# Row maxima by 64-row products, probability sums on GpSimd alone, and the division in four pieces, in a 16-head attention on one core

## What is computed

```python
x = layernorm(x + L0_attn(x))   # a test-time-trained attention, 8 chunks of 256 tokens
x = layernorm(x + L0_ffn(x))    # 8 experts, top-1 routing with a capacity
x = layernorm(x + L1_attn(x))   # softmax attention, the part that the change touches
x = layernorm(x + L1_ffn(x))    # 8 gated experts, top-1, and a shared one

def L1_attn(x):                 # 16 heads of 64, s = 2048
    q, k, v = (x @ W).reshape(b, s, 16, 64) for W in (Wq, Wk, Wv)
    dot = einsum('bihd,bkhd->bhik', q, k)
    w = softmax(dot / sqrt(64))
    return einsum('bhij,bjhd->bihd', w, v).reshape(b, s, 1024) @ Wo + bo
```

## Time and profile before

| what | us |
|---|---|
| median of 3 runs (1936.26 to 1939.78) | 1939.38 |
| profiled execution | 1943.69 |
| its span, from first to last instruction | 1942.4 |
| TensorE busy (matmul) | 1715.7 (88%) |
| VectorE busy | 1404.4 (72%) |
| GpSimd busy | 1094.9 (56%) |
| ScalarE busy | 774.3 (40%) |

### The profile page before, as it was taken

The page is one execution under the profiler, slowest core; times in us unless marked ns, Lnnn a source line. Parts: engine busy times, 40 slices in busy tenths (PEclk is TensorE's granted clock), DMA queues, the critical chain, the costliest instruction groups (busy, mean ns, idle before and its releaser), DMA issues.

```text
span 1942.4 us, 35745 instructions
## 1 busy us (share of the span) xinstructions
PE 1715.7 (88%) x13785; PEld 935.6 (48%) x13785; DVE 1404.4 (72%) x2509; ACT 774.3 (40%) x1175; POOL 1094.9 (56%) x644
## 2 busy tenths in 40 slices
PE   5877852848999999999999999999999999996793
PEld 4766641834444444444444444444444444443473
DVE  3576546567787777877777877777788788877575
ACT  2454430423444444444444444434344444442221
POOL 2232202233777777776777777767677777775303
PEclk9978755869999999999999999999999999998797
DMA  7000000210000000000000000000000000002212
GB/s 234 3 3 4 3 1 17 62 29 1 1 1 1 1 1 1 1 1 1 1 1 1 1 1 1 1 1 1 1 1 1 1 1 1 1 1 65 64 41 61
DMA packets 35199, 29.77 MB, mean 15 GB/s; under 512 B 4060, under 2 KB 30928, under 8 KB 35032
## 3 DMA queue, kind: packets, MB, share of 16 engines
q1 hardware_dynamic: 27064, 20.28, 3.6%
q0 software_dynamic: 2048, 4.20, 0.7%
q10 hardware_dynamic: 5920, 3.01, 0.5%
HBM read 18.31 MB, written 9.18 MB: 14 GB/s over the span
## 4 chain that ended last, share of the span: by engine, by line
PE 81%; DVE 9%; issue 5%; POOL 4%; DMA 1%; ACT 1%; SPq 0%; DVEq 0%; POOLq 0%; ACTq 0%
PE psum L1774 23%; PE psum L1759 20%; PE psum L1733 8%; PE psum L1753 6%; PE psum L1789 2%; PE psum L1783 2%; PE psum L1404 2%; PE psum L1706 1%; DVE a_mx L1937 1%; PE psum L1365 1%; PE psum L1180 1%; PE psum L1192 1%; POOL a_acc L2068 1%; PE psum L447 1%; PE psum L452 1%
## 5 line engine op out<-in xcount | busy, mean ns | idle before, releaser
L2068 POOL TENSOR_TENSOR a_acc<-a_acc,a_Pb 128x832 f32<-128x832 f32 x448 | 892.7, 1993 | 311.2 <-ACT a_Pb L1876 277.3
L1937 DVE TENSOR_REDUCE a_mx<-psum 128x2 f32<-128x1024 f32 x512 | 625.7, 1225 | 237.3 <-PE psum L1733 234.3
L1876 ACT ACTIVATE a_Pb<-psum 128x1024 f32<-128x1024 f32 x512 | 496.8, 1022 | 704.4 <-PE psum L1759 701.4
L1774 PE MATMUL psum<-a_Pb,a_Vb 128*64 128x512 f32 x2048 | 494.1, 603 | 0.0
L1988 DVE TENSOR_TENSOR a_acc<-a_acc,a_Pb 128x192 f32<-128x192 f32 x448 | 232.6, 519 | 28.2 <-ACT a_Pb L1876 5.0
L1774 PEld LDWEIGHTS psum<-a_Pb,a_Vb 128*64 128x64 f32 x2048 | 127.0, 136 | 244.5 <-issue 173.6
L1733 PE MATMUL psum<-a_Kh,a_Qh 64*128 64x512 f32 x1024 | 230.9, 447 | 10.6 <-DVE a_mx L1937 10.5
L1759 PE MATMUL psum<-a_Qh,a_Kh 64*128 64x512 f32 x1024 | 231.0, 446 | 0.0
L1733 PEld LDWEIGHTS psum<-a_Kh,a_Qh 64*128 64x128 f32 x1024 | 97.0, 184 | 225.4 <-issue 214.5
L1759 PE MATMUL psum<-a_Ql,a_Kh 64*128 64x512 f32 x1024 | 203.8, 393 | 0.0
L1759 PE MATMUL psum<-a_Qh,a_Kl 64*128 64x512 f32 x1024 | 203.0, 391 | 0.0
(11 more groups left out here) (375 smaller groups left out, 1950.8 us busy)
## 6 DMA issues: line engine op xcount, KB each, us to landing
x_rows<-zero ACTq DMA_DIRECT2D x2, 1472.0 KB, 16.4
g_w<-in_L_ffn_w_eDF_dram SPq DMA_DIRECT2D x2, 1408.0 KB, 9.6
r_W<-in_L_ffn_W_dram SPq DMA_DIRECT2D x1, 2048.0 KB, 11.4
r_tile_x<-x_rows SPq DMA_DIRECT2D x23, 64.0 KB, 1.9
y_rows<-r_tile_y SPq DMA_DIRECT2D x23, 64.0 KB, 1.5
g_tile_x<-x_rows SPq DMA_DIRECT2D x23, 64.0 KB, 1.9
y_rows<-g_tile_y SPq DMA_DIRECT2D x23, 64.0 KB, 1.5
g_w<-in_L_ffn_w_eFD_dram SPq DMA_DIRECT2D x2, 512.0 KB, 11.3
```

Source lines behind the costliest of these rows:

```text
L1774: last = pe.matmul(ps[HEAD[h], B_O, :], b.Vb[:, p // 2 % 2, kc, at], b.Pb[:, step % BUFS, h * QT:(h + 1) * QT], start=(kc == 0), stop=(kc ...
L1876: act.activation(b.Pb[:, step % BUFS, :], ps[:, slot:slot + 2, :].rearrange("p a b -> p (a b)"), ACT.Exp, scale=SCALE).then_inc(S["probs"], 1)
L1937: v.tensor_reduce(b.mx[:, :, qc, quarter:quarter + 1], ps[:, bank:bank + 2, :], AX.X, ALU.max).then_inc(S[f"free{bank}"], 1)
L2068: g.tensor_tensor(b.acc[:, u, at], before, b.Pb[:, step % BUFS, at], ALU.add).then_inc(S["added_pool"], 1)
```

## The change

- The ones products: instead of four of 32 rows for a round there are two of 64 rows for each tile of keys, ahead of that tile's scores, one for each head. The first pair waits for the first probabilities of the round before, the second for the second. Mr and its mask then hold four rows at 0 and four at 64, and negate writes nm once, not twice.
- The constant POOL = 832 goes. VectorE adds nothing any more, and GpSimd adds all 1024 columns, 15 times in a unit. One semaphore, added, replaces two.
- The division is done in four pieces of 128 columns. They stand at the ends of rounds 3, 5, 6 and 7 on VectorE; the reciprocals are in rounds 2 to 5, ahead of the early maximum. At the very end each piece follows its reciprocal.
- The sums of U - 1 are taken in round 1 instead of 2, the output of U - 2 in round 2 instead of 1.
- Two waits of VectorE on its own semaphores are added (negated, normalised).

```diff
--- before.py
+++ after.py
@@ -1552,7 +1552,6 @@
 RN = NT // 2
 ROUNDS = UNITS * RN
 STEPS = 2 * ROUNDS
-POOL = 832
 BUFS = 8
 SCALE = 1.0 / float(np.sqrt(D))
 B_O, B_M, B_P = 4, 5, 7
@@ -1564,10 +1563,10 @@
     p, qt = U // NU, U % NU
     if d == 0 and p < PAIRS - 1:
         return "k", p + 1, qt
-    if d == 1 and U > 1:
+    if d == 1 and U:
+        return "sum", U - 1
+    if d == 2 and U > 1:
         return "out", U - 2
-    if d == 2 and U:
-        return "sum", U - 1
     if d == 3 and p // 2 < PAIRS // 2 - 1:
         return "v", p // 2 + 1, U % RN
     if d == 4 and U < UNITS - 2:
@@ -1746,14 +1745,13 @@
             freed(("mask", U))
             freed(("q", U))
             freed(("k", p, NU - 1))
-        if R:
-            pe.wait_ge(S["probs"], 2 * R)
-        for g in range(4):
-            rows = slice(32 * g, 32 * (g + 1))
-            pe.matmul(ps[:, 2 * (g % 2) + g // 2, :], b.ones[rows, :], b.Mr[rows, :], start=True, stop=False, tile_position=(32 * g, 0))
         for i in range(2):
             kc, slot = 2 * d + i, 2 * i
             at = slice(kc * P, (kc + 1) * P)
+            if R:
+                pe.wait_ge(S["probs"], 2 * R - 1 + i)
+            for h in range(2):
+                pe.matmul(ps[:, slot + h, :], b.ones[HEAD[h], :], b.Mr[HEAD[h], :], start=True, stop=False)
             for n, (K, Q) in enumerate(((b.Kh, b.Qh), (b.Kh, b.Ql), (b.Kl, b.Qh))):
                 for h in range(2):
                     last = pe.matmul(ps[:, slot + h, :], K[HEAD[h], p % 2, at], Q[HEAD[h], U % 3, :], start=False, stop=(n == 2))
@@ -1776,15 +1774,14 @@
             last.then_inc(S["weighted"], 1)
 
     def sums(U):
-        pe.wait_ge(S["added_dve"], 15 * (U + 1))
-        pe.wait_ge(S["added_pool"], 15 * (U + 1))
+        pe.wait_ge(S["added"], 15 * (U + 1))
         bank = begin(("sum", U))
         for h in range(2):
             last = pe.matmul(ps[HEAD[h], bank, :], k.ones[:, 0:D], b.acc[:, U % 2, h * QT:(h + 1) * QT], start=True, stop=True)
         end(last, bank)
 
     def output(U):
-        pe.wait_ge(S["normalised"], U + 1)
+        pe.wait_ge(S["normalised"], 4 * U + 4)
         bank = begin(("out", U))
         end(pe.matmul(ps[:, bank, :], k.att_o[:, U // NU, :], b.On[:, :], start=True, stop=True), bank)
 
@@ -1871,14 +1868,13 @@
         act.wait_ge(S["scores"], step + 1)
         if step >= BUFS:
             act.wait_ge(S["weighted"], step - BUFS + 1)
-            act.wait_ge(S["added_dve"], adds_of(step - BUFS))
-            act.wait_ge(S["added_pool"], adds_of(step - BUFS))
+            act.wait_ge(S["added"], adds_of(step - BUFS))
         act.activation(b.Pb[:, step % BUFS, :], ps[:, slot:slot + 2, :].rearrange("p a b -> p (a b)"), ACT.Exp, scale=SCALE).then_inc(S["probs"], 1)
 
     def heads_out(U):
         act.wait_ge(S["weighted"], NT * (U + 1))
         if U > 1:
-            act.wait_ge(S["normalised"], U - 1)
+            act.wait_ge(S["normalised"], 4 * U - 4)
         act.activation(b.Or[:, U % 2, :], ps[:, B_O, :], ACT.Copy).then_inc(S["heads_out"], 1)
 
     stores_done(act, k, 0)
@@ -1934,6 +1930,8 @@
     def maximum(U, m):
         quarter, qc = m // 4, m % 4
         bank = begin(("max", U, m))
+        if U and m == 0:
+            v.wait_ge(S["negated"], U)
         v.tensor_reduce(b.mx[:, :, qc, quarter:quarter + 1], ps[:, bank:bank + 2, :], AX.X, ALU.max).then_inc(S[f"free{bank}"], 1)
 
     def negate(U):
@@ -1943,10 +1941,8 @@
         if U:
             bank, n = plan.at["mask", U - 1]
             v.wait_ge(S[f"full{bank}"], n)
-        for half in range(2):
-            nm = b.nm[:, :].rearrange("p (h x) -> p h x", h=2)[:, :, 32 * half:32 * half + 4]
-            last = v.tensor_reduce(nm, b.mx[:, :, :, :], AX.X, ALU.max, negate=True)
-        last.then_inc(S["negated"], 1)
+        nm = b.nm[:, :].rearrange("p (h x) -> p h x", h=2)[:, :, 0:4]
+        v.tensor_reduce(nm, b.mx[:, :, :, :], AX.X, ALU.max, negate=True).then_inc(S["negated"], 1)
 
     def mask(U):
         bank = begin(("mask", U))
@@ -1954,18 +1950,21 @@
                         ALU.mult).then_inc(S[f"free{bank}"], 1)
 
     def invert(U, part):
+        if U and part == 0:
+            v.wait_ge(S["normalised"], 4 * U)
         bank, n = plan.at["sum", U]
         v.wait_ge(S[f"free{bank}"], n)
         at = slice(part * P, (part + 1) * P)
         v.reciprocal(b.rec[:, at], b.ssum[:, at]).then_inc(S["inverted"], 1)
 
-    def normalise(U):
-        v.wait_ge(S["inverted"], 4 * U + 4)
+    def normalise(U, part):
+        v.wait_ge(S["inverted"], 4 * U + part + 1)
         v.wait_ge(S["heads_out"], U + 1)
-        if U:
+        if U and part == 0:
             bank, n = plan.at["out", U - 1]
             v.wait_ge(S[f"full{bank}"], n)
-        v.tensor_tensor(b.On[:, :], b.rec[:, :], b.Or[:, U % 2, :], ALU.mult).then_inc(S["normalised"], 1)
+        at = slice(part * P, (part + 1) * P)
+        v.tensor_tensor(b.On[:, at], b.rec[:, at], b.Or[:, U % 2, at], ALU.mult).then_inc(S["normalised"], 1)
 
     def output(U):
         qt = U % NU
@@ -1975,25 +1974,12 @@
         yq = k.y_all[:, 4 * qt:4 * qt + 4, :]
         v.tensor_tensor(yq, ps[:, bank, :].rearrange("p (a d) -> p a d", a=4), yq, ALU.add).then_inc(S[f"free{bank}"], 1)
 
-    def add(step):
-        U, kc = step // NT, step % NT
-        u, at = U % 2, slice(POOL, 2 * QT)
-        v.wait_ge(S["probs"], step + 1)
-        if kc > 1:
-            v.wait_ge(S["added_dve"], adds_of(step - 1))
-        elif U > 1:
-            bank, n = plan.at["sum", U - 2]
-            v.wait_ge(S[f"full{bank}"], n)
-        before = b.Pb[:, (step - 1) % BUFS, at] if kc == 1 else b.acc[:, u, at]
-        v.tensor_tensor(b.acc[:, u, at], before, b.Pb[:, step % BUFS, at], ALU.add).then_inc(S["added_dve"], 1)
-
     stores_done(v, k, 0)
     v.memset(b.mask[:, :, :], 0.0)
     dve.did(v.memset(b.nm[:, :], 0.0))
     dve.wait()
-    for g in range(4):
-        rows = slice(32 * g, 32 * (g + 1))
-        dve.did(v.tensor_copy(b.mask[rows, :, :], bcast(k.ident[rows, 32 * g:32 * g + 4].unsqueeze(2), [32, 4, P])))
+    for h in range(2):
+        dve.did(v.tensor_copy(b.mask[h * D:h * D + 32, :, :], bcast(k.ident[h * D:h * D + 32, h * D:h * D + 4].unsqueeze(2), [32, 4, P])))
     gather_norm_dve(k, 0, k.y_all, k.x_all, 1)
     v.wait_ge(S["relu_small"], 64)
     v.wait_ge(S["normed"], 8)
@@ -2019,25 +2005,19 @@
             maximum(*late[1:])
         if d == 7 and U < UNITS - 1:
             negate(U + 1)
-        if R:
-            if (R - 1) % RN:
-                add(2 * R - 2)
-            add(2 * R - 1)
+        if U and 2 <= d <= 5:
+            invert(U - 1, d - 2)
         if early:
             maximum(*early[1:])
         key = misc_job(R)
         if key and key[0] in ("q", "k", "mask", "out"):
             {"q": queries, "k": keys, "mask": mask, "out": output}[key[0]](*key[1:])
-        if U and 3 <= d <= 6:
-            invert(U - 1, d - 3)
-        if U and d == 7:
-            normalise(U - 1)
-    for step in (STEPS - 2, STEPS - 1):
-        add(step)
+        if U and d in (3, 5, 6, 7):
+            normalise(U - 1, (3, 5, 6, 7).index(d))
     output(UNITS - 2)
     for part in range(4):
         invert(UNITS - 1, part)
-    normalise(UNITS - 1)
+        normalise(UNITS - 1, part)
     output(UNITS - 1)
 
 
@@ -2057,15 +2037,15 @@
 
     def add(step):
         U, kc = step // NT, step % NT
-        u, at = U % 2, slice(0, POOL)
+        u = U % 2
         g.wait_ge(S["probs"], step + 1)
         if kc == 1 and U > 1:
             bank, n = plan.at["sum", U - 2]
             g.wait_ge(S[f"full{bank}"], n)
         if step > 1:
-            g.wait_ge(S["added_pool"], adds_of(step - 1) if kc > 1 else 15 * U)
-        before = b.Pb[:, (step - 1) % BUFS, at] if kc == 1 else b.acc[:, u, at]
-        g.tensor_tensor(b.acc[:, u, at], before, b.Pb[:, step % BUFS, at], ALU.add).then_inc(S["added_pool"], 1)
+            g.wait_ge(S["added"], adds_of(step - 1) if kc > 1 else 15 * U)
+        before = b.Pb[:, (step - 1) % BUFS, :] if kc == 1 else b.acc[:, u, :]
+        g.tensor_tensor(b.acc[:, u, :], before, b.Pb[:, step % BUFS, :], ALU.add).then_inc(S["added"], 1)
 
     for step in range(STEPS):
         if step % NT:
```

## The result

The changed kernel takes 1923.12 us (median of 4 runs, 1922.02 to 1924.77) beside 1939.18 for the kernel before; the ratio is 0.9924 (95% interval 0.9908 to 0.994). On another chip it was 1924.51 and 0.9919 (0.9893 to 0.9946). The forecast was 1922.5. TensorE's granted clock is 1.00, the 2.4 GHz level, from 458 to 1700 us before and after.

What follows compares the result with a forecast made beforehand. TensorE was taken to bound the kernel, with VectorE and GpSimd having room. From 1943.7 profiled, loop -20.3, waits -5.7 and end +5 gave 1922.7; forecast 1922.5 us, range 1896 to 1956.

Steps and rivals of the forecast that it cites:

- Products over 64 rows: TensorE's round: two changes of row height go, one pair is added; early maximum at 2.19 instead of 2.36, 0.175 less.
- rival E: GpSimd becomes the bound, needing more than 2.6 us per add instead of 2.36; about 1945 and up; chance 0.05.
- The pieces: Division on VectorE in rounds 3, 5, 6, 7: pieces wait for GpSimd's adds; PE loses 0.65 of 1.40 per unit.
- The walk: Timing of a steady unit from each late maximum: PE loses 0.46 in round 7 and 0.19 in round 0.
- Rivals B: Division pieces slip past GpSimd without being blocked, taking 0.28; 1900 us; chance 0.19.
- C: Slower: same blocking in a worse phase, over 1.23 us lost per unit; half way 1963, up to some 2010; chance 0.27.
- Units 24 to 30: Shorter rounds, GpSimd lags more: losses of 1.0 for units 24 to 27, 1.1 for 28 and 29, 1.9 for 30.
- The loop: Attention loop, all units: 1.4 + 17.2 + 4 x 0.4 + 2 x 0.3 - 0.5, 20.3 us faster.
- The end: Last unit: GpSimd's last ten adds cost +4, the division in four pieces +1, together +5 us.
- The 5.7 of waits before: PE's four waits for VectorE's maxima, 500 to 1600 us: 5.7 us gained in the profiled execution, 1.4 against the median.
- The sum: Whole kernel: profiled 1943.7 - 20.3 - 5.7 + 5, or median 1939.4 - 20.3 - 1.4 + 5, both 1922.7.
- Rival D: TensorE: pairs cost their passes and height changes are not regained; + 59 us, near 2000; chance 0.05.

Runs made afterwards that it cites:

- pieces between the maxima: Changed kernel with division pieces and reciprocals exchanged, pieces between late and early maximum in rounds 3, 4 (two) and 5: 1896.76 us, ratio 0.9796.
- pieces with one input: Changed kernel with each division piece replaced by a reduction from the weighted values alone, multiplication by reciprocals left out: 1892.88 us, ratio 0.9775.

## Why the prediction was right, point by point

- **Products over 64 rows: right, with a price slightly low.** 0.175 a round was forecast, 0.19 measured. The first step in 64 rows is 0.34 (0.33 forecast) and the rest 0.23 (0.232 forecast).
- **GpSimd's add: right.** 2.36 forecast, 2.379 measured, 2.52 from start to start instead of 2.50. It is not the bound of a steady unit (rival E falls).
- **The pieces: right in place, somewhat low in size.** The walk put the loss into rounds 7 and 0 (0.46 and 0.19, early maxima at 2.65 and 2.38); measured are 2.68 and 2.31, and round 0 loses some more behind the early maximum, it lasts 5.51 against 5.30 in the kernel with the pieces between the maxima, and round 7 5.39 against 4.80. Loss of a unit: 40.82 - 40.02 = 0.80, with 0.65 forecast. The sign named for it was missed: some 20 us of waits of PE for maxima were forecast, and the profile shows 10.0 from 500 to 1600 us. The walk's 0.65 is lateness, read from starts, and the profile counts idle time alone (0.33 in the row of 898.93, where the maximum is 0.51 late). The pieces with one input show that it is the second input, and the pieces between the maxima that it is the place. Rivals B (no block) and C (over 1.23 a unit) fall for the changed kernel. C's mechanism is what happens in the 64-row products alone.
- **Units 24 to 30: mixed.** Units 24 to 27 lost 1.2 us each, not 1.0; 28 and 29 1.2, not 1.1. Unit 30 gained 1.1 (38.16 to 37.1) where the walk had it 0.5 slower: its pieces in rounds 5, 6 and 7 took 0.28, 0.82 and 1.84, so the one that the walk had starting in the same instant as GpSimd's add, 3.77, came first. That is the walk at its limit, and worth 1.6 us.
- **The loop: 20.3 forecast, 17.1 measured** without the disturbed units. The 0.10 by which a steady unit was mis-sized makes 2.
- **The end: term mis-sized, 5 forecast, 7.1 measured.** I had GpSimd enter the last ten adds 0.5 late and took 25.0 for them. It is without a pause from the unit's second add on (14 in 35.21), and the wait of PE is 7.46. Splitting the division: +1.2 for +1.
- **The 5.7 of waits before** I put down to the profiled execution. They lie in the disturbed units above, which are worth 7.8. Whether other executions of the kernel before lack them is open, as none was profiled beside it.
- **The sum: close in part by luck.** For the profiled executions 21.0 was forecast (20.3 + 5.7 - 5) and 18.9 came: loop and end were 3.2 and 2.1 too good, the disturbed units were worth 7.8 rather than 5.7, and the loop began 1.1 earlier, which I had not forecast. Between the medians 16.7 was forecast and 16.1 measured. Of this, loop and end give 17.1 - 7.1 = 10.0 by the traces, where I had 20.3 - 5 = 15.3. The other 6 us must come from disturbed units in the executions before and from what lies ahead of the loop; no run here divides them. So two terms were too good by 5.3 together, and something that I had put at 1.4 made up for it.
- **Rival D** (no price on a change of row height) falls with the 32-row products in the changed kernel. That the lost time belongs to the change of height, and not to a quad of 32 rows as such, is a reading of the steps; no run tells the two apart.

The Trainium skill (SBUF — State Buffer, Who interferes with whom) limits the exclusion to VectorE operations with two SBUF inputs or in a mode that takes both ports. The 275 ns of the piece with one input, and reciprocals that stay at 0.94 in all kernels here, agree with it.

## What to carry to other kernels

Where GpSimd is nearly always busy, count VectorE's operations with two SBUF inputs as waits until the end of a GpSimd operation, and put each where VectorE would idle anyway (26 to 30 us here). Shortening the bounding engine moves all these meetings, so an edit that is right by itself (the 64-row products, 0.19 us in a round) can lose 18 us where a gain of some 43 was estimated, until the other queue is freed. And look at the last unit separately: engines that have lost their work there can take over the bound's.

## What I had not expected of the hardware

The size of the interaction: 64-row products shorten nearly every round by 0.19, and a single VectorE add of 192 columns (0.35 alone) that asks 0.03 us behind a GpSimd start instead of 0.17 ahead of it makes round 6 1.5 us longer. One such meeting in a unit takes back the whole gain of the other rounds, and two or three in each of the units 24 to 30 make the kernel slower than before. One quad of 32-row products, a single pass of 512 columns, between 64-row pairs cost 2 x 0.232 + 0.19 = 0.65 us, nearly as much as three pairs: 0.44 for its own step, and some 0.1 more on the step ahead of it (0.43 instead of 0.34) and on the one behind (0.33 instead of 0.23).
